# Decoder of four layers on one core: context block of the latent attentions padded to full height, and a new order of ranking, loads, output ring and final sums in the two mixture stages

## Chip, core and metric

One core of a Trainium2 chip runs the whole program in one launch. The metric is the device time in microseconds. TensorE (PE) multiplies, VectorE (DVE), ScalarE (ACT) and GpSimd (POOL) work on rows in SBUF and PSUM, and SyncE (SP) issues most of the loads; GpSimd issues the indirect transfers.

## The reference, cut to what matters

The residual x has 4 batches of 512 tokens with 256 features. It passes twelve stages, four layers of attention, cross-attention and feed-forward, each of the form x = x + f(layernorm(x)). Three of them (the cross-attentions of layers 1, 2 and 3; 16, 16 and 8 heads of 64) let the tokens attend to themselves and to 64 rows of context:

```
kv = concat([tokens, context]) @ Wkv          # 512 + 64 rows
attn = softmax(q @ k.T)                       # 512 x 576 per head and batch
out  = attn @ v                               # the product at issue in the first part of the change
```

Two of them (the feed-forward of layers 2 and 3) are mixtures of eight experts with two experts for each token:

```
gate = sigmoid or softmax of the two best of 8 router scores
h    = relu(x W1)^2                 # layer 2: 512 hidden features
h    = silu(x W1 + b1) * (x W2 + b2)  # layer 3: 512 + 512 up features, with biases
out  = sum over the two experts of gate * (h W_down [+ b3])
```

## The kernel before

**Stages.** Each stage is one block in which every engine runs its own written-out program; the engines meet only through semaphores, and a stage begins when all engines have left the one before. Stage 4, 7 and 10 (function `latent_attention`) take about 605 to 1341, 1950 to 2737 and 3149 to 3593 us of the profile; stages 8 and 11 (`sparse_experts`, called by `l2_ffn` and `l3_ffn`) take 2737 to 3000 and 3593 to 3940 us.

**Latent attention.** For each batch and each pair of heads (80 pairs in the three stages: 32, 32 and 16) TensorE does four "spots" of 128 query rows. In a spot it multiplies scores (L2491, rows of 64, so tiles of 64x128), transposes the shares of an earlier spot (L2411, L2423), and does one piece of other work: values (L2346), output projection (L2358), or `attended` (L2441, L2444). `attended` sums shares times values over five blocks of keys: blocks 0 to 3 hold 128 tokens each, and each of the two heads writes 64 of the 128 rows of PSUM bank 6 (tiles of 128x64, L2441). The fifth block is the 64 rows of context. `turn_context_probs` has put the shares of head 0 on partitions 0 to 63 and those of head 1 on 64 to 127 of `pTc`, and `vc` (context_values) holds the values the same way, so each head multiplies 64 rows by 64 columns (tiles of 64x64, L2444). In the trace each multiplication in float32 is two records (two passes). The order is part 0: blocks 0 and 1; part 1, one spot later: blocks 2, 3 and the context. The values in `vc` are copied by ScalarE at L2583.

**Mixture stages.** The tokens are 16 tiles of 128: group 0 has 4 tiles and group 1 has 12. Each group is ranked by itself: `pick` marks the two best experts (DVE), `rank` counts places with matmuls on PE (L4376, L4378), `put` makes the row indices and the expert of each sorted tile (DVE), `weigh` the gates. GpSimd then scatters the normed rows into DRAM by expert (`scatter`, L4298: 8 transfers for group 0 and 24 for group 1). SP loads the sorted rows back in chunks of three tiles (`load_sorted`, L4264; for a group it waits for that group's scatters at L4257 to L4260). There are 46 sorted tiles in each stage, 15 of group 0 and 31 of group 1. For tile n TensorE does `project_up(n)` (L4404, 16 records in layer 2, 32 in layer 3), `project_down(n-1)` (L4420) and `turn_rows(n+2)` (L4390). ScalarE moves turned rows (L4482), copies the expert's up weights out of the stage's weights (`copy_weights`, L4494) and applies relu or silu. DVE squares or multiplies (`make_hidden`) and moves the result into a ring `y` of RY = OUTPUT_RING = 4 row buffers (`make_rows`, L4678, L4681); GpSimd scatters a ring entry to the token's place (`scatter_rows`, L4307) and tells it by `stored`. While group 1 is being scattered, one `scatter_rows` stands behind every three scatters of rows, 8 in all. `rank(1)` stands on PE after `project_up(1)`, and `put(1)`, `weigh(1)` on DVE after `make_hidden(1)`, ahead of `make_rows(0)`. `pick(1)` is ahead of the loop.

**Loads.** SP issues the router, five small tables, the bias columns (layer 3), the up weights (4 MB in layer 2, 8 MB in layer 3), the stage's rows (layer 3: the down bias, 1 MB) and the down weights (4 MB), and only then waits for the scatters. DVE waits for both biases ahead of its loop.

**End.** When all 46 tiles are stored, SP fetches the expert outputs back (L4269; one batch earlier in the loop, three at the end), and `combine` adds the two halves of each token tile with two DVE instructions in a row (L4686, L4689), 12 tiles at the end. In layer 3 the result is stored by batch.

## Time and profile before

| what | value |
|---|---|
| time, median of 3 runs | 3911.28 us (3911.06 to 3914.19) |
| the profiled execution | 3942.55 us |
| its span | 3940.4 us, granted TensorE clock 0.929 |
| busy: PE / DVE / ACT / POOL | 3495.3 / 2191.8 / 1495.8 / 1370.0 us |
| PE busy, stage 4 from 656 to 1335 us | 657.24 of 679 us |
| stage 8 | 2737 to 3000 us |
| stage 11 | 3593 to 3940 us |

A row of the timeline gives start, length, engine, line, operation, the tiles written and read, the number of records merged (x) and in brackets how long the engine had been idle and what ended it. PEclk in the table by windows is the granted clock as a share of 2.4 GHz: 1.00 is 2.4 GHz and 0.50 is 1.2 GHz. "issue" and "remote" name idle time for which the profile shows no partner.

### The profile page before, as it was taken

Reading aid. Unit: us, or ns where it says so; the run is one execution under the profiler, and the core shown is the slowest. Engines: PE = TensorE matmul, PEld = TensorE weight load, DVE = VectorE, ACT = ScalarE, POOL = GpSimd, SP = SyncE. Lnnn points to the kernel's source line nnn. Section 1 sums busy time; section 2 is a strip of 40 time slices with the busy share of each in tenths; the row PEclk is TensorE's granted clock in tenths of the full one; section 3 lists DMA queues with packets and bytes.
Section 4 is the critical chain, followed back from the end, with each engine's and each line's share of the span. In section 5 each row is a group of like instructions: output and inputs, shape, how many; then the busy total and the mean of one; then the engine's idle time right before and its main releaser. Section 6 shows DMA issues by size and latency. Waiting matters only on the chain. (4 is left out here: it accounts for less than half of the span.)

```text
span 3940.4 us, 54458 instructions
## 1 busy us (share of the span) xinstructions
PE 3495.3 (89%) x18930; PEld 2240.6 (57%) x18930; DVE 2191.8 (56%) x5367; ACT 1495.8 (38%) x3040; POOL 1370.0 (35%) x1904
## 2 busy tenths in 40 slices
PE   7998897899999977888798999998896989995997
PEld 5675684445555566344444555555794445554896
DVE  5374444645556468666367676765234466664454
ACT  3253112433434364233244444443352144442453
POOL 2141441423323255232254444533422144442311
PEclk9999978999999988899799999999798889996998
DMA  2004001000000000000100000001221000003212
GB/s 100 1 1 123 14 1 46 1 1 1 1 1 1 13 1 24 1 1 1 49 1 1 1 1 1 1 1 76 99 80 57 4 25 1 1 1 160 71 60 84
DMA packets 48718, 108.85 MB, mean 28 GB/s; under 512 B 6660, under 2 KB 32900, under 8 KB 46404
## 3 DMA queue, kind: packets, MB, share of 16 engines
q1 hardware_dynamic: 40964, 84.88, 6.3%
q0 software_dynamic: 7488, 20.49, 1.5%
q8 instruction: 158, 2.59, 0.3%
q14 instruction: 108, 0.88, 0.1%
HBM read 70.67 MB, written 34.68 MB: 27 GB/s over the span
## 5 line engine op out<-in xcount | busy, mean ns | idle before, releaser
L2653 POOL TENSOR_SCALAR probs<-probs,inv_sum 128x512 f32<-128x512 f32 x640 | 437.7, 697 | 1008.3 <-DVE inv_sum L2774 1008.1
L2616 ACT ACTIVATE probs<-psum_banks,neg_max 128x576 f32<-128x576 f32 x640 | 468.5, 737 | 742.5 <-DVE neg_max L2857 742.5
L2857 DVE TENSOR_REDUCE neg_max<-psum_banks 128x1 f32<-128x576 f32 x640 | 455.0, 752 | 213.4 <-PE psum_banks L2491 206.8
L2491 PE MATMUL psum_banks<-keys_T,queries_T 64*128 64x288 f32 x2560 | 406.0, 436 | 52.5 <-ACT probs L2616 43.2
L2783 DVE COPY probs_T<-psum_banks 128x512 f32<-128x512 f32 x640 | 409.2, 681 | 4.5 <-PE psum_banks L2411 4.5
L2491 PEld LDWEIGHTS psum_banks<-keys_T,queries_T 64*128 64x128 f32 x2560 | 224.5, 189 | 269.2 <-ACT probs L2616 147.9
L2411 PE MATMUL psum_banks<-ident,probs 128*128 128x128 f32 x2560 | 356.5, 283 | 3.2 <-POOL probs L2653 2.3
L2411 PEld LDWEIGHTS psum_banks<-ident,probs 128*128 128x128 f32 x2560 | 280.3, 143 | 128.2 <-POOL probs L2653 63.3
L2441 PE MATMUL psum_banks<-probs_T,values 128*64 128x512 f32 x1280 | 310.9, 607 | 2.2 <-issue 2.2
L4404 PE MATMUL psum_banks<-sorted_T,tile_weights 128*128 128x128 f32 x2208 | 270.1, 279 | 9.2 <-ACT tile_weights L4494 4.9
L4404 PEld LDWEIGHTS psum_banks<-sorted_T,tile_weights 128*128 128x128 f32 x2208 | 262.2, 196 | 10.7 <-issue 10.6
L2853 DVE TENSOR_TENSOR psum_banks<-psum_banks,key_mask 128x128 f32<-128x128 f32 x192 | 57.5, 299 | 280.1 <-PE psum_banks L2491 280.1
L4420 PE MATMUL psum_banks<-w_L_experts_down,hidden_T 128*128 x736 | 183.3, 394 | 19.4 <-DVE expert_rows L4678 8.7
L4307 POOL DMA_INDIRECT expert_outputs<-expert_rows,output_index x92 | 90.3, 982 | 297.4 <-DVE expert_rows L4681 126.7
L2665 POOL TENSOR_TENSOR square_sum<-square_sum,neg_half 128x8 f32<-128x8 f32 x102 | 167.1, 1639 | 70.8 <-DVE square_sum L2749 69.3
L4420 PEld LDWEIGHTS psum_banks<-w_L_experts_down,hidden_T 128*128 128x128 f32 x736 | 137.4, 197 | 37.7 <-issue 21.7
L2346 PE MATMUL psum_banks<-w_L_xattn_Wkv,batch_normed_T 128*128 128x512 f32 x320 | 158.7, 620 | 0.0
L2441 PEld LDWEIGHTS psum_banks<-probs_T,values 128*64 128x64 f32 x1280 | 78.8, 136 | 133.8 <-issue 124.1
L4494 ACT COPY tile_weights<-w_L_experts_up 128x1024 f32 (+1 forms) x92 | 135.3, 1472 | 23.5 <-issue 23.5
L1962 ACT ACTIVATE probs_T<-psum_banks 128x512 f32<-128x512 f32 (+3 forms) x128 | 83.0, 701 | 127.7 <-PE psum_banks L1899 126.9
L2656 POOL TENSOR_TENSOR context_probs<-probs,inv_sum 128x128 f32<-128x128 f32 x320 | 128.9, 403 | 0.0
L2616 ACT ACTIVATION_READ_ACCUMULATOR probs<-psum_banks,neg_max 128x1 f32 x640 | 125.4, 196 | 0.0
(535 smaller groups left out, 6119.2 us busy)
## 6 DMA issues: line engine op xcount, KB each, us to landing
normed<-sorted_rows SPq DMA_DIRECT2D x30, 385.5 KB
sorted_rows<-zero_rows SPq DMA_DIRECT2D x8, 1028.0 KB, 14.5
w_L_experts_down<-in_L_experts_down SPq DMA_DIRECT2D x2, 4096.0 KB, 37.1
normed<-expert_outputs SPq DMA_DIRECT2D x8, 1024.0 KB, 7.9
w_L_xattn_Wkv<-in_L_xattn_Wkv SPq DMA_DIRECT2D x2, 2048.0 KB, 8.5
w_L_experts_up<-in_L_experts_up SPq DMA_DIRECT2D x1, 4096.0 KB, 13.0
sorted_rows<-zero_rows SPq DMA_DIRECT2D x4, 899.5 KB, 14.1
x_res<-in_x SPq DMA_DIRECT2D x4, 512.0 KB, 6.9
```

Source lines behind the costliest of these rows:

```text
L2346: last = pe.matmul(k.ps[:, 7, :], rows, wkv[:, c, W + a * 512:W + (a + 1) * 512], start=c == 0, stop=c == KC - 1)
L2411: last = pe.transpose(k.ps[:, 4 + n % 2, c * P:(c + 1) * P], prob[:, (b * NS + s) % PB, at + c * P:at + (c + 1) * P], k.ident[:, :])
L2441: last = pe.matmul(k.ps[r, 6, :], values[:, b % VB, c, (2 * j + h) * 64:(2 * j + h + 1) * 64], pT[:, q % 2, h, c, :], start=c == 0, stop=F ...
L2491: last = pe.matmul(k.ps[:, 2 * h + a, 0:HALF], qT[r, b % 2, j, t * P:(t + 1) * P], kT[r, j, k0:k0 + HALF], start=True, stop=True)
L2616: act.activation(prob[:, g % PB, h * w:(h + 1) * w].rearrange("p (a n) -> p a n", a=2), k.ps[:, 2 * h:2 * h + 2, 0:HALF], ACT.Exp, bias=nm ...
L2653: pool.tensor_scalar(w, w, inv[:, g % 4, h:h + 1], 1.0, ALU.mult, ALU.mult).then_inc(shared, 1)
L2665: pool.tensor_tensor(ss[:, i % 4, 2, :], ss[:, i % 4, 1, :], k.half[:, 0:8], ALU.pow).then_inc(inverted, 1)
L2783: dve.tensor_copy(pT[:, q % 2, h, :, t * P:(t + 1) * P], k.ps[:, 4 + n % 2, :].rearrange("p (c q) -> p c q", q=P)).then_inc(copied, 1)
L2857: dve.tensor_reduce(nmax[:, g % 4, h:h + 1], k.ps[:, 2 * h:2 * h + 2, 0:HALF], AX.XY, ALU.max, negate=True).then_inc(maxed, 1)
L4404: last = pe.matmul(ps[:, 2 * (n % 2) + part, f * P:(f + 1) * P], wt[:, n % 2, c, part * 512 + f * P:part * 512 + (f + 1) * P], xsT[:, n % ...
L4420: last = pe.matmul(ps[:, 6, 0:D], h[:, n % 2, f * P:(f + 1) * P], w_down[:, f // F, f % F * D:f % F * D + (E - 1) * STEP + D][:, bass.ds(a ...
L4494: act.copy(wt[:, n % 2, :, :], w_up[:, :, 0:(E - 1) * STEP + UP][:, :, bass.ds(at, UP)]).then_inc(weights_copied, 1)
```

## The change

In the latent attentions `vc` gets a second copy for each head, of full height: `vc[:, h]` holds the context values of head h on its own 64 partitions and zeros on the other 64. Two DVE memsets write the zeros at the start of the stage, and PE waits once for them. The context is then multiplied like the other blocks: all 128 rows of `pTc` against `vc[:, h]`.

In the mixture stages: `rank(1)` follows `project_up(0)`; `put(1)` follows `make_hidden(0)`; `weigh(1)` follows `make_rows(1)`. ScalarE copies the weights of tiles 0 and 1 ahead of the sigmoid or exp of group 1. The ring has six buffers. In layer 3 SP issues the down bias and the down weights behind the first two loads of sorted rows, and the waits for the biases stand at their first use. In the 12 sums at the end DVE adds the first half, ScalarE scales the second half in place and GpSimd adds it.

```diff
-        vc = k.sb("context_values", [P, PAIRS, NC], st)
+        vc = k.sb("context_values", [P, 2, PAIRS, NC], st)
...
+                        if q == 0:
+                            pe.wait_ge(zeroed, 2)
...
-                                last = pe.matmul(k.ps[r, 6, :], vc[r, j, :], pTc[r, q % 2, :], start=False, stop=True)
+                                last = pe.matmul(k.ps[r, 6, :], vc[:, h, j, :], pTc[:, q % 2, :], start=False, stop=True)
...
-                            act.copy(vc[r, 4 * a:4 * a + 4, :], k.ps[r, 7, :].rearrange(
+                            act.copy(vc[r, h, 4 * a:4 * a + 4, :], k.ps[r, 7, :].rearrange(
...
                 batch_aggr(0)
+                for h in range(2):
+                    dve.memset(vc[64 - 64 * h:128 - 64 * h, h, :, :], 0.0).then_inc(zeroed, 1)
                 dve.wait_ge(ctx_loaded, 16)
...
-OUTPUT_RING = 4
+OUTPUT_RING = 6
...
-                    sp.dma_start(columns[:, :, :, :], columns.src[:, :, :, :]).then_inc(bias_loaded, 16)
+                    sp.dma_start(columns[:, :, :, :], columns.src[:, :, :, :]).then_inc(columns_loaded, 16)
                 sp.dma_start(w_up[:, :, :], w_up.src[:, :, :]).then_inc(up_loaded, 16)
-                for w in k.stage_rows:
-                    sp.dma_start(w.dst[:, :], w.src).then_inc(bias_loaded, 16)
-                sp.dma_start(w_down[:, :, :], w_down.src[:, :, :]).then_inc(down_loaded, 16)
+                def load_late_weights():
+                    for w in k.stage_rows:
+                        sp.dma_start(w.dst[:, :], w.src).then_inc(bias_loaded, 16)
+                    sp.dma_start(w_down[:, :, :], w_down.src[:, :, :]).then_inc(down_loaded, 16)
+                if bias is None:
+                    load_late_weights()
...
                 load_sorted(0)
                 load_sorted(1)
+                if bias is not None:
+                    load_late_weights()
...
                 for n in range(done, NTILES):
                     scatter_rows(n)
+                for t in range(TT, NT):
+                    pool.wait_ge(halfway, t + 1)
+                    pool.wait_ge(second_scaled, t - TT + 1)
+                    pool.tensor_tensor(k.x[:, t, :], k.x[:, t, :], got[:, t - TT, 1, :], ALU.add).then_inc(combined, 1)
...
                     if n < NTILES:
                         project_up(n)
-                    if n == 1:
+                    if n == 0:
                         rank(1)
...
                 for p in range(1, PIECES):
                     move_piece(p)
+                copy_weights(0)
+                copy_weights(1)
                 if from_sigmoid:
...
                 move_rows(0)
                 move_rows(1)
-                copy_weights(0)
-                copy_weights(1)
...
+                for t in range(TT, NT):
+                    act.wait_ge(fetched[t // TT], 16)
+                    act.mul(got[:, t - TT, 1, :], got[:, t - TT, 1, :], gate[:, 1, t:t + 1]).then_inc(second_scaled, 1)
...
+                    if t >= TT:
+                        return
                     dve.wait_ge(halfway, t + 1)
...
-                if bias is not None:
-                    dve.wait_ge(bias_loaded, 32)
...
-                    if n == 1:
+                    if n == 0:
                         put(1)
-                        weigh(1)
                     if n >= 1:
                         make_rows(n - 1)
+                    if n == 2:
+                        weigh(1)
```

## Rows read from the trace of the kernel before

**Rows 1.** Timeline of PE, stage 4: part 0, then part 1 of `attended`

```profile
1011.31 1.94 PE L2441 MATMUL psum_banks<-probs_T,values 128*64 128x512 f32 x8
1013.18 1.24 PE L2491 MATMUL psum_banks<-keys_T,queries_T 64*128 64x288 f32 x8
...
1017.10 1.94 PE L2441 MATMUL psum_banks<-probs_T,values 128*64 128x512 f32 x8
1018.96 1.08 PE L2444 MATMUL psum_banks<-context_probs_T,context_values 64*64 64x512 f32 x4
1019.97 1.24 PE L2491 MATMUL psum_banks<-keys_T,queries_T 64*128 64x288 f32 x8
```

**Rows 2.** Timeline of PE, stage 10: sixteen passes of 512 columns with one tile shape

```profile
3262.65 7.13 PE L2369 MATMUL psum_banks<-w_L_xattn_Wq,batch_normed_T 128*128 128x512 f32 x16
```

**Rows 3.** Waits of PE, stage 4 (us in total, times, longest)

```profile
PE psum_banks L2491 <- ACT probs L2616: 14.1, 9, 2.4
```

**Rows 4.** Timeline of DVE: start of stage 4, and a memset in stage 8

```profile
609.38 1.40 DVE L2822 BATCH_NORM_STATS2 context_stat<-probs_T 64x6 f32<-64x256 f32 x4 [1.87 <-DMA probs_T<-in_ctx_rows]
...
2741.83 0.14 DVE L4619 MEMSET gate_row<- 128x96 f32 x1
```

**Rows 5.** Timeline of POOL and SP: last scatter of group 0, first sorted load, stages 8 and 11

```profile
2764.98 0.97 POOL L4298 DMA_INDIRECT sorted_rows<-normed,row_index  x1 [0.30 <-issue]
2767.80 50.04 SPq L4264 DMA_DIRECT2D normed<-sorted_rows  x5
...
3621.01 0.97 POOL L4298 DMA_INDIRECT sorted_rows<-normed,row_index  x1 [0.30 <-issue]
3635.36 78.42 SPq L4264 DMA_DIRECT2D normed<-sorted_rows  x6
```

**Rows 6.** Stage 11 by windows: stretch, length, busy of PE, PEld, DVE, ACT, POOL, PEclk, DMA share, GB/s

```profile
3630.00:3634.00 4.00, 0.00 (x0) 0.00 (x0) 0.00 (x0) 0.00 (x0) 0.00 (x0) 0.50 0.57 229
```

**Rows 7.** Timeline of ACT and PE: exp of group 1, first tiles of stage 11

```profile
3629.41 0.28 ACT L4476 ACTIVATE gate_exp<-gate_exp 128x96 f32<-128x96 f32 x1 [7.67 <-DVE gate_exp L4550]
3638.68 0.66 PE L4390 MATMUL psum_banks<-ident,normed 128*128 128x128 f32 x2 [13.31 <-DMA normed<-sorted_rows]
3643.26 5.49 PE L4404 MATMUL psum_banks<-sorted_T,tile_weights 128*128 128x128 f32 x32 [2.76 <-ACT tile_weights L4494]
...
3666.57 4.07 PE L4404 MATMUL psum_banks<-sorted_T,tile_weights 128*128 128x128 f32 x32
```

**Rows 8.** Timeline of PE, stage 8: first tiles, then two steady starts

```profile
2774.98 3.75 PE L4404 MATMUL psum_banks<-sorted_T,tile_weights 128*128 128x128 f32 x16 [2.13 <-ACT tile_weights L4494]
...
2781.35 2.76 PE L4378 MATMUL psum_banks<-gate_mask,ones 128*128 128x96 f32 x24
...
2790.64 3.77 PE L4420 MATMUL psum_banks<-w_L_experts_down,hidden_T 128*128 x8 [2.69 <-DVE expert_rows L4678]
...
2794.64 3.01 PE L4404 MATMUL psum_banks<-sorted_T,tile_weights 128*128 128x128 f32 x16
...
2813.55 1.95 PE L4404 MATMUL psum_banks<-sorted_T,tile_weights 128*128 128x128 f32 x16
...
2817.29 1.95 PE L4404 MATMUL psum_banks<-sorted_T,tile_weights 128*128 128x128 f32 x16
```

**Rows 9.** Timeline of ACT, stage 8, while group 1 is scattered

```profile
2803.28 0.60 ACT L4509 ACTIVATE hidden_T<-psum_banks 128x512 f32<-128x512 f32 x1 [6.73 <-remote]
```

**Rows 10.** Timeline of DVE and POOL: last sums of the program, and additions elsewhere

```profile
3925.20 0.48 DVE L4686 SCALAR_TENSOR_TENSOR x_res<-normed,gate_weights,x_res 128x256 f32<-128x256 f32 x1 [8.84 <-DMA normed<-expert_outputs]
...
3935.81 0.48 DVE L4689 SCALAR_TENSOR_TENSOR x_res<-normed,gate_weights,x_res 128x256 f32<-128x256 f32 x1
...
541.75 1.31 DVE L3316 SCALAR_TENSOR_TENSOR x_res<-projected,out_rstd,x_res 128x256 f32<-128x256 f32 x2
...
545.01 0.64 POOL L3185 TENSOR_TENSOR keys_decayed<-keys_decayed,gate_products 128x256 f32<-128x256 f32 x1
...
602.65 1.67 DVE L3316 SCALAR_TENSOR_TENSOR x_res<-projected,out_rstd,x_res 128x256 f32<-128x256 f32 x4 [0.17 <-DVE projected L3308]
```

More of the change, by code:

```diff
@@ L2267, in latent_attention @@
         with signals(nc, "ctx_stat", "ctx_aggr", "ctx_shift", "ctx_rstd", "ctx_normed", "ctx_turned", "ctx_ready",
-                     "ctx_loaded", "mask_made", "stats", "aggr", "shift", "rstd", "normed", "norm_turned", "norm_moved",
+                     "ctx_loaded", "mask_made", "zeroed", "stats", "aggr", "shift", "rstd", "normed", "norm_turned", "norm_moved",
                      "made", "act_moved", "dve_moved", "squared", "summed", "floored", "inverted", "scaled", "turned",
                      "moved", "placed") as (
-                ctx_stat, ctx_aggr, ctx_shift, ctx_rstd, ctx_normed, ctx_turned, ctx_ready, ctx_loaded, mask_made, stats, aggr,
+                ctx_stat, ctx_aggr, ctx_shift, ctx_rstd, ctx_normed, ctx_turned, ctx_ready, ctx_loaded, mask_made, zeroed, stats, aggr,
                 shift, rstd, normed, norm_turned, norm_moved, made, act_moved, dve_moved, squared, summed, floored,
@@ L4217, in sparse_experts @@
                      "router_loaded", "small_loaded", "up_loaded", "bias_loaded",
-                     "down_loaded", "next_ids") as (
+                     "down_loaded", "next_ids", "columns_loaded") as (
                 stats, aggr, shift, rstd, offset, normed, ids_set, copied_again, turned, ready, scored, rowed, picked,
                 exped, masked, ranked, indexed, placed, order, router_loaded, small_loaded, up_loaded, bias_loaded,
-                down_loaded, next_ids), signals(
+                down_loaded, next_ids, columns_loaded), signals(
                 nc, "sorted_0", "sorted_1", "ids_spared", "ids_taken", "x_turned", "x_moved", "up", "up_linear",
                 "shifted", "silued", "linear_read", "hidden_made", "weights_copied", "down", "rows_made", "combined",
-                "halfway", "x_stored", *[f"fetched_{b}" for b in range(B)]) as (
+                "halfway", "second_scaled", "x_stored", *[f"fetched_{b}" for b in range(B)]) as (
                 sorted_0, sorted_1, ids_spared, ids_taken, x_turned, x_moved, up, up_linear, shifted, silued, linear_read,
-                hidden_made, weights_copied, down, rows_made, combined, halfway, x_stored,
+                hidden_made, weights_copied, down, rows_made, combined, halfway, second_scaled, x_stored,
                 *fetched), nc.Block() as block:
@@ L4468, in _ @@
                                    scale=rs[:, 1, t:t + 1]).then_inc(normed, 1)
-                for p in range(1, PIECES):
-                    move_piece(p)
-                if from_sigmoid:
-                    act.wait_ge(scored, PIECES)
-                    act.activation(row[:, tiles_of[1], 0:E], scores[1], ACT.Sigmoid).then_inc(rowed, 1)
-                else:
-                    act.wait_ge(picked, 2)
-                    act.activation(e[:, tiles_of[1], :], e[:, tiles_of[1], :], ACT.Exp).then_inc(exped, 1)
                 def move_rows(n):
@@ L4495, in copy_weights @@
                         weights_copied, 1)
+                for p in range(1, PIECES):
+                    move_piece(p)
+                copy_weights(0)
+                copy_weights(1)
+                if from_sigmoid:
+                    act.wait_ge(scored, PIECES)
+                    act.activation(row[:, tiles_of[1], 0:E], scores[1], ACT.Sigmoid).then_inc(rowed, 1)
+                else:
+                    act.wait_ge(picked, 2)
+                    act.activation(e[:, tiles_of[1], :], e[:, tiles_of[1], :], ACT.Exp).then_inc(exped, 1)
                 move_rows(0)
                 move_rows(1)
-                copy_weights(0)
-                copy_weights(1)
                 for n in range(NTILES):
@@ L4652, in make_hidden @@
                         return
+                    if n == 0:
+                        dve.wait_ge(columns_loaded, 16)
                     at = dve.value_load(bias_at[0:1, 0, n:n + 1], min_val=0, max_val=(E - 1) * 8)
@@ L4679, in make_rows @@
                     else:
+                        if n == 0:
+                            dve.wait_ge(bias_loaded, 16)
                         at = dve.value_load(bias_at[0:1, 1, n:n + 1], min_val=0, max_val=(E - 1) * D)
@@ L4698, in _ @@
                         make_hidden(n)
-                    if n == 1:
+                    if n == 0:
                         put(1)
-                        weigh(1)
                     if n >= 1:
                         make_rows(n - 1)
+                    if n == 2:
+                        weigh(1)
                     if GROUP_SORTED[0] + 10 <= n < GROUP_SORTED[0] + 10 + TT:
```

## The prediction

> **What bounds the kernel now.** I first looked for the stages that the change touches, then asked in each which engine has no idle time. In the latent attentions TensorE bounds: its timeline goes from one product to the next without a bracket [rows 1], and its longest wait in stage 4, for ScalarE's exponentials, is 14.1 us in 9 places [rows 3], nearly all at the start of a batch. A microsecond of TensorE is there a microsecond of the stage. In the mixture stages I read three stretches apart. At the start, TensorE waits for the sorted rows and then for the first weight copies [rows 5, 7, 8]. In the middle it is the bound again, with a start of `project_up` every 2817.29 - 2813.55 = 3.74 us in stage 8 [rows 8]; in stage 11, which has twice the up products, a tile should take 5.52 us (3.74 us and 16 more records of an up product, which take 1.95 us less a pipe's length of 0.17). Only while group 1 is scattered does it stand still here and there. At the end DVE alone adds 12 tiles, (3935.81 + 0.48) - 3925.20 = 11.1 us [rows 10], with every other engine idle.
>
> **The context as a fifth block.** The number of matmuls, their columns and their passes stay the same; what changes is the tile shape of the last two passes, from 64x64 to the 128x64 of the eight records before. Part 1 now takes 1019.97 - 1017.10 = 2.87 us from its start to the next score: 1.86 us for the four paired passes and 1.01 us for the two of the context [rows 1]. Passes of 512 columns in one shape cost at most 7.13 / 16 = 0.446 us each [rows 2], and part 0, four such passes and one change of shape, takes 1.87 us [rows 1]. Part 1 after the change is part 0 and two passes more: 1.87 + 2 x 0.43 = 2.73 us (0.43 is 7.13 less a pipe's length of 0.6, over 15). That is 0.14 to 0.15 us less per pair, and 80 pairs give 12 us. Part 1 stands in the longest spot of its four, so the exponentials of that spot have more time than elsewhere and the gain should not turn into a wait; if every one of the shortened spots were held up by the exponentials instead, about a third would stay. Bounds 4 to 13, value **-12.0 us**. The zeros: a memset of 96 columns takes 0.14 us [rows 4], and one of 512 columns at the same rate at most 5 times that, 0.7 us. Both lie in front of DVE's wait for the context load, 1.87 us long [rows 4], so they cost **nothing**; were the load early they would cost up to 1.4 us a stage. The wait of TensorE for them is over 50 us late by then.
>
> **Stage 8, start.** The first up product waits 2.13 us for the weight copies behind the two moved rows [rows 8]. The copies need `placed(0)` and the up weights, both there before the sigmoid of group 1, so they move into ScalarE's idle time and the product begins when the second tile is turned: **-2.1 us** (0 if the copies were late).
>
> **Stage 8, second ranking.** `put(1)` and `weigh(1)` on DVE stand in front of `make_rows(0)`, for which the second down product waits 2.69 us [rows 8]. The idle time costs twice: behind it that down product takes 3.77 us and the up product 3.01 us, against 1.95 us for an up product in the steady stretch [rows 8], the clock having fallen from 2.4 to 1.2 GHz. From the first up product to the fourth it is 2794.64 - 2774.98 = 19.7 us [rows 8]. After the change the order is up 0 (3.75 less the pipe, 3.55, at 1.2 GHz as now), ranking (2.8 [rows 8], and 0.6 of slow clock), a turn (0.2), and two steady tiles (2 x 3.74), in all 14.6 us. `put(1)` is 16 small DVE instructions of 0.2 to 0.4 us, 3.6 us from the ranking's end; TensorE has up 1 and down 0 to do meanwhile, 3.6 us, and `make_rows(0)` is needed only for down 1. `weigh(1)`, 2.3 us behind `make_rows(1)`, meets the up product of tile 3. So nothing new is late: **-5.0 us** (bounds 2.7, the idle time alone, and 5.9, idle time and slow records).
>
> **Stage 11, start.** This is the largest term. In stage 8 the first sorted load is issued 2767.80 - 2764.98 = 2.8 us after the last scatter of group 0 began; in stage 11 it takes 3635.36 - 3621.01 = 14.35 us [rows 5]. In between the DMA engines still move 229 GB/s while every compute engine stands still [rows 6]: up weights, row biases and down weights, 13.4 MB, are ahead. Without the last two, 5.2 MB or two fifths of it, some 14 of the 38 us of traffic go, and the load should be issued 2.8 us after the last scatter as in stage 8, at 3623.8, its rows on chip 3.3 us later (3638.68 - 3635.36 [rows 5, 7]), at 3627.1. Then something else is last: `move_rows` stands behind the exp of group 1, whose input comes from DVE, and which ends at 3629.7 [rows 7]. From there it is a move and the second turn, 1.1 us, to an up product at 3630.8 instead of 3643.26 [rows 7]. The copies of 1.9 us each are hidden before the exp. **-12.4 us**, and -6 if the scatters still land half as late as now. What is moved: the two late loads go behind two waits of SP, and land at about 3624.9 + 14 = 3639; down 0 comes at 3630.8 + 5.3 + 2.8 + 0.2 + 3.6 = 3642.7, 4 us later. No other load waits behind them before tile 6.
>
> **Stage 11, second ranking.** From the first to the fourth up product 3666.57 - 3643.26 = 23.3 us [rows 7]; after the change 5.3 (the 5.49 us of up 0 less the pipe) + 2.8 + 0.2 + 2 x 5.52 = 19.4 us: **-3.9 us** (bounds 2.2 and 4.1).
>
> **Ring of six.** In neither stage does DVE wait for a buffer now: while group 1 is scattered GpSimd needs 4 x (0.97 + 0.30) = 5.1 us for each ring entry [rows 5], DVE hands one over at that pace or slower. It would matter only if TensorE ran through the scatters undisturbed at 3.74 us a tile. **0** (bound: -5).
>
> **The stretch of the scatters.** ScalarE stands still up to 6.73 us with all its inputs there [rows 9], and the tiles of this stretch lose some 19 us in stage 8 and 8 us in stage 11 against the steady pace. What it waits for the profile doesn't show, and the change takes none of these transfers away, so I leave it at **0**, with -15 and +10 as bounds, since other instructions will meet the scatters.
>
> **Sums on three engines.** DVE's part falls to 0.42 us a tile, but GpSimd's addition of a tile takes 0.64 us alone [rows 10]. Side by side they are not free: two DVE additions that meet GpSimd's take 1.31 us where four alone take 1.67 us [rows 10], so one of them was held up by 0.47 us. If they take turns throughout it is 12 x (0.42 + 0.64) = 12.7 us against 11.1, +1.5 us a stage; if they overlap, 0.5 + 12 x 0.64 = 8.2, -2.9 us. I take the first, as both rows' lengths speak for it: **+3.0 us** for both stages (bounds -5.8 and +4.6).
>
> The Trainium skill (SBUF — State Buffer, "SBUF: two separate sides") says that an addition of VectorE with two inputs in SBUF and any GpSimd instruction hold a shared port for the whole instruction and exclude each other. The stretched rows agree; by it and GpSimd's longer additions the sum would be about a microsecond a stage worse.
>
> **Sum.** -12.0 - 2.1 - 5.0 - 12.4 - 3.9 + 3.0 = -32.4 us. The profiled execution has 3942.55 us, 2.15 more than its span and 31.3 more than the median; its forecast is 3910. The terms are intervals between waits and not shares, so I take them from the median as they are: 3911.3 - 32.4 = 3878.9.
>
> **Rivals.** (a) The late weights are not what holds the scatters. Each scatter would then land as late as now, and stage 11 would gain only the hidden copies, 2.8 us [rows 7], instead of 12.4: 3888.5. For it: GpSimd's scatters are another queue. Against it: 14.35 against 2.8 us with the same eight scatters [rows 5], and an end that comes with the end of the traffic [rows 6].
>
> By the Trainium skill (DMA: Bandwidth & Descriptors, "Queues, rings and completion order") a DMA engine takes its queues in turn, packet by packet. With equal turns a scatter would not be held by the weights, which is this rival; the 14.35 us speak against it, unless a turn of the weights moves much more than one of the scatter.
>
> (b) The stalls in the scatters belong to the old order and go: another 15 to 25 us, 3859. For it: TensorE will be ahead by then. Against: ScalarE's 6.73 us have no partner in the old order either.
> (c) The latent attentions turn the gain into waits for the exponentials: 3887.
> (d) Slower: with six buffers TensorE runs ahead of GpSimd's 5.1 us a tile in stage 8, and idles in every tile until the clock falls to 1.2 GHz for the stretch, as behind the 2.69 us of rows 8. A tile then takes 7.5 instead of 3.74 us, and 12 tiles cost 45 us: 3924. [...]
> (e) The sums overlap fully: 3870.
>
> **How the numbers follow.** Forecast 0.55, (a) 0.10, (b) 0.12, (c) 0.10, (d) 0.03, (e) 0.07, the rest (a smaller gain from several bounds at once, within 7.8 us of before) 0.03. The range takes in (a), (c), (e) and the edge of (b), and the open stretch of the scatters: 3860 to 3896. Within 0.2%, 7.8 us, a measurement of this kernel can't tell a change. Faster 0.94, same 0.03, slower 0.03.
>
> **What would show it.** One kind of tile 128x64 in `attended` and 2.7 us from part 1 to the next score; the first sorted load of stage 11 some 3 us after the last scatter began; no wait of 2 us at the second down product; up 0 directly behind the second turn; GpSimd's additions at the end stretched to 1 us or more. Wrong it would be if TensorE showed new waits for L2616 in the latent attentions, if down 0 of stage 11 waited for its weights, or if the scatters' stalls moved onto TensorE's path.

## The result, and the profile after

The changed kernel takes 3895.01 us (median of 5 runs, 3892.15 to 3897.32), the kernel before in the same runs 3914.19 us (3911.06 to 3918.84): a ratio of 0.9949, 95% interval 0.9938 to 0.9960, or 19.2 us less. The forecast was 32.4 us less. The range (3860 to 3896) held by 1 us, the size was 13 us too large, and this part is mostly about these 13 us.

The profiled execution of the changed kernel took 3895.01 us and spans 3893.3. That of the kernel before spans 3940.4, so the two traces are 47 us apart and the medians 19. This is the first thing to explain. The page after begins so (section 1 is busy time by engine, then the granted clock in 40 slices):

```profile
span 3893.3 us, 54516 instructions
PE 3471.5 (89%) x18930; PEld 2243.6 (58%) x18930; DVE 2192.1 (56%) x5349; ACT 1506.5 (39%) x3064; POOL 1392.1 (36%) x1928
...
PEclk9999978999999988899889999999898889997998
```

**Latent attentions.** Timeline of PE in stage 4, against [rows 1]. Part 1 now lasts 1015.50 - 1012.77 = 2.73 us up to the next score, the forecast 2.73; the wait for the exponentials is unchanged from [rows 3]:

```profile
1012.77 1.94 PE L2443 MATMUL psum_banks<-probs_T,values 128*64 128x512 f32 x8
1014.54 1.03 PE L2446 MATMUL psum_banks<-context_probs_T,context_values 128*64 128x512 f32 x4
1015.50 1.24 PE L2493 MATMUL psum_banks<-keys_T,queries_T 64*128 64x288 f32 x8
...
PE psum_banks L2493 <- ACT probs L2618: 14.1, 9, 2.4
```

The zeros take 0.48 us each on DVE, and the wait for the context behind them, 1.87 us in [rows 4], still has 0.46 us left, so they cost nothing (timeline of DVE, stage 4):

```profile
607.88 0.48 DVE L2823 MEMSET context_values<- 64x512 f32 x1 [0.16 <-issue]
608.83 1.40 DVE L2826 BATCH_NORM_STATS2 context_stat<-probs_T 64x6 f32<-64x256 f32 x4 [0.46 <-DMA probs_T<-in_ctx_rows]
```

**Stage 8.** Timeline of PE, against [rows 8]. The first up product follows the second turn, the ranking comes behind it, and the waits of 2.13 and 2.69 us are gone. But at tile 15, the first of group 1, there is a new wait for the sorted rows, and the up product behind it takes 3.23 us in place of 1.95:

```profile
2764.36 0.69 PE L4405 MATMUL psum_banks<-ident,normed 128*128 128x128 f32 x2 [0.46 <-ACT sorted_T L4488]
2764.84 3.62 PE L4419 MATMUL psum_banks<-sorted_T,tile_weights 128*128 128x128 f32 x16
2768.26 0.59 PE L4391 MATMUL psum_banks<-gate_mask,w_before_token 128*128 128x104 f32 x2
...
2824.00 0.69 PE L4405 MATMUL psum_banks<-ident,normed 128*128 128x128 f32 x2 [3.75 <-DMA normed<-sorted_rows]
2824.48 3.23 PE L4419 MATMUL psum_banks<-sorted_T,tile_weights 128*128 128x128 f32 x16
```

That load is issued when the scatters of group 1 have landed, and POOL issued the last of them at 2817.70, one instruction every 1.28 us:

```profile
2816.42 0.98 POOL L4309 DMA_INDIRECT sorted_rows<-normed,row_index  x1 [0.30 <-issue]
2817.70 0.97 POOL L4309 DMA_INDIRECT sorted_rows<-normed,row_index  x1 [0.30 <-issue]
```

**Stage 11.** Timelines of POOL, SP, ACT and PE, against [rows 5, 7]. The first sorted load is issued 3596.53 - 3592.53 = 4.0 us after the last scatter of group 0, in place of 14.35; SP's wait for the scatters' landing, which ends just ahead of it, lasts 27.8 us in place of 37.2. The exp of group 1 is then last, and the move and the turn follow it; down 0, for the late weights, waits for nothing:

```profile
3592.53 0.98 POOL L4309 DMA_INDIRECT sorted_rows<-normed,row_index  x1 [0.30 <-issue]
3596.53 0.91 SPq L4273 DMA_DIRECT2D normed<-sorted_rows  x2
3602.72 0.28 ACT L4512 ACTIVATE gate_exp<-gate_exp 128x96 f32<-128x96 f32 x1 [4.08 <-DVE gate_exp L4568]
3603.32 0.69 PE L4405 MATMUL psum_banks<-ident,normed 128*128 128x128 f32 x2 [2.59 <-ACT sorted_T L4488]
3603.80 6.13 PE L4419 MATMUL psum_banks<-sorted_T,tile_weights 128*128 128x128 f32 x32
3616.42 1.89 PE L4435 MATMUL psum_banks<-w_L_experts_down,hidden_T 128*128 x8
```

**The sums.** End of stage 8: timelines of DVE and POOL, then what the sequencers recorded where the stage's block ends (columns: instruction, count, duration in ns as minimum, median and maximum, first and last start in us), then SP's first load of stage 9:

```profile
2957.22 9.53 DVE L4708 SCALAR_TENSOR_TENSOR x_res<-normed,gate_weights,x_res 128x256 f32<-128x256 f32 x12 [9.05 <-DMA normed<-expert_outputs]
2957.88 10.14 POOL L4359 TENSOR_TENSOR x_res<-x_res,normed 128x256 f32<-128x256 f32 x12 [7.90 <-ACT normed L4530]
...
L4231 POOLq DRAIN  x1: 7678/7678/7678, 2966.8 to 2966.8; - x1
L4231 DVEq DRAIN  x1: 17/17/17, 2968.3 to 2968.3; - x1
L4231 SPq EVENT_SEMAPHORE  x1: 17/17/17, 2974.6 to 2974.6; - x1
...
2975.72 0.35 SPq L3902 DMA_DIRECT2D w_L_attn_w_q<-in_L_attn_w_q  x1
```

The sums end at 2968.0, 10.8 us after their start, against 11.1 us in [rows 10]. The next stage begins 7.7 us later. In between POOL executes one DRAIN of 7.68 us. It stands behind the last addition in POOL's program and begins at 2966.8. The instruction is in the kernel before too. There it begins right behind the last scatter and is over before DVE has added its first tile, which began at 2987.4 (the same view of the kernel before, end of stage 8):

```profile
L4227 POOLq DRAIN  x1: 7635/7635/7635, 2979.2 to 2979.2; - x1
L4227 DVEq DRAIN  x1: 17/17/17, 2998.8 to 2998.8; - x1
```

### The profile page after: what moved, and what is told of

Same layout as the page of the kernel before. It is cut to its first block and busy times, and to the rows that moved or that the text cites. A ratio compares the mean times of both kernels' runs of the same rounds, so it can differ in the third digit from the quotient of the medians.

```text
span 3893.3 us, 54516 instructions
## 1 busy us (share of the span) xinstructions
PE 3471.5 (89%) x18930; PEld 2243.6 (58%) x18930; DVE 2192.1 (56%) x5349; ACT 1506.5 (39%) x3064; POOL 1392.1 (36%) x1928
## 5 line engine op out<-in xcount | busy, mean ns | idle before, releaser
L4435 PE MATMUL psum_banks<-w_L_experts_down,hidden_T 128*128 x736 | 174.3, 380 | 2.2 <-DVE expert_rows L4703 1.4
## 6 DMA issues: line engine op xcount, KB each, us to landing
w_L_experts_up<-in_L_experts_up SPq DMA_DIRECT2D x1, 4096.0 KB, 12.2
```

Source lines behind the costliest of these rows:

```text
L4435: last = pe.matmul(ps[:, 6, 0:D], h[:, n % 2, f * P:(f + 1) * P], w_down[:, f // F, f % F * D:f % F * D + (E - 1) * STEP + D][:, bass.ds(a ...
```

## The experiments

The runs come in four groups, each on another chip (in this order those numbered 9, 4, 12 and 10). In the second and fourth the kernel before took 3914 us, in the first and third 3942 and 3939. I call these places B and A; the medians on record belong to B, the profiled execution of the kernel before to A. What in the chips differs isn't shown.

I measure a stage by its length, from SP's first load of it to SP's first load of the next (rows are shown for two kernels below). All in us:

```
kernel                    place  stage 4  7      10     8      11     whole, median
before (first profile)    A      735.3  787.4  444.1  262.8  346.9
before again              A      735.3  787.4  444.1  262.9  346.0  3940.98
context alone             A      730.7  782.3  439.7  262.5  345.5  3929.12
late loads alone          A      735.0  786.8  444.2  262.7  334.9  3929.86
late loads alone          B      735.3  786.8  444.4  241.8  329.3  3900.30
second ranking alone      A      738.0  786.8  439.5  255.7  337.9  3927.50
changed kernel            B      731.1  782.4  439.9  246.7  328.4  3894.17
 ring of four             B      730.7  782.3  440.1  245.9  328.2  3895.87
 sums on one engine       B      730.7  782.7  440.3  242.9  322.8  3888.25
 ranking as before        B      730.2  783.0  440.1  250.5  333.2  3907.88
 loads as before          A      730.6  782.9  440.0  261.2  340.7  3927.51
 one engine, sparser rows A      730.7  782.6  440.8  259.3  338.2  3914.52
```

**1. The kernel before again: are the stalls one execution's?** No edit.

> The kernel before, unchanged, profiled a second time. Theory S (the stalls without a partner in the scatter stretches, about 19 us in stage 8 and 8 us in stage 11, belong to the one profiled execution and not to the ordinary ones): this profile's span is 3910 to 3918 us, its stage 8 lasts some 244 to 247 us where the first profile had 262.75, its stage 11 some 338 where it had 346.9, and its up projections in the scatter stretch follow one another without gaps. Rival R (the stalls belong to the kernel before and the change removed them): the second profile shows stages 8 and 11 at about 262 and 347 us again. Ratio to itself 1.000 for both.

3940.98 us, ratio to itself 0.9994 (0.9985 to 1.0004). The stalls are there again, in the same places and sizes; timeline of ACT in stage 8 of this run, against [rows 9]:

```profile
2804.65 0.60 ACT L4509 ACTIVATE hidden_T<-psum_banks 128x512 f32<-128x512 f32 x1 [7.08 <-remote]
2830.43 0.37 ACT L4482 COPY sorted_T<-psum_banks 128x256 f32<-128x256 f32 x1 [4.35 <-remote]
```

So theory S falls, and rival R looked right. But here the timed runs were 3941 us too. Neither theory had thought of that: the stalls go with where the kernel is run.

**2. The context block alone.** On the kernel before:

```
-        vc = k.sb("context_values", [P, PAIRS, NC], st)
+        vc = k.sb("context_values", [P, 2, PAIRS, NC], st)
...
-    last = pe.matmul(k.ps[r, 6, :], vc[r, j, :], pTc[r, q % 2, :], start=False, stop=True)
+    last = pe.matmul(k.ps[r, 6, :], vc[:, h, j, :], pTc[:, q % 2, :], start=False, stop=True)
```

> The kernel before with the padded context block of the latent attentions alone. Forecast step: -12.0 us (ratio 0.9969, bounds -4 to -13). Theory M (the attentions gave what was forecast, the shortfall lies in the mixture stages): -11 to -13 us, that is ratio 0.9967 to 0.9972. Rival (part of the attention's gain is given back in the stages behind it): -5 to -8 us, ratio 0.9980 to 0.9987.

Ratio 0.9967 (0.9954 to 0.9979), 13.0 us less. Stages 4, 7 and 10 are 4.6, 5.1 and 4.4 us shorter, 14.1 in all. Theory M holds.

**3. The late loads alone, in both places.**

```
+                def load_late_weights(): ...
                 load_sorted(0)
                 load_sorted(1)
+                if bias is not None:
+                    load_late_weights()
```

> The kernel before with the bias rows and the down projection's weights of stage 11 issued behind the first two sorted loads, alone. Forecast step: -12.4 us (ratio 0.9968). The two profiles show 11.0 us from the stage's start to the first up product, some of it from the earlier copies of the weights: -9 to -12 us by them, ratio 0.9970 to 0.9977. Rival (in ordinary executions the scatters land sooner than in the profiled one, so that less was to be gained): -3 to -6 us, ratio 0.9985 to 0.9992.

Ratio 0.9971 (0.9959 to 0.9983), 12.2 us less, in A. The first up product of stage 11 comes 39.9 us after the stage's start in place of 49.8. That is 9.9 us; what lies between it and the last down product is 2.2 us shorter as well (269.5 against 271.7), for which no cause is shown.

> The kernel before with the late loads of stage 11 alone, a second time. Where the kernel before takes 3914 us: its stage 8 is the unchanged one, and by the kernel with the old ranking (250.5 us) less the 6.1 us that the drain cost there it should last 244 to 245 us, so that the changed kernel's 246.7 us are 2 us more than before; its stage 11 should last 329 to 331 us (333.2 less the 3.7 us of the drain) against some 341 without the late loads, and the whole should come out 10 to 13 us below the kernel before. Rival (the step is worth less without the stalls): 4 to 8 us below. Where the kernel before takes 3940 us: 12 us below, as in the first run of this kernel, with stage 11 at 335 us.

Ratio 0.9970 (0.9958 to 0.9982), 14.2 us less, in B. The step is worth the same in both places, and this kernel shows what the places differ in. Its stage 8, which the edit doesn't touch, lasts 2997.98 - 2735.29 = 262.7 us in A and 2974.75 - 2732.92 = 241.8 us in B (timelines of SP, first A, then B):

```profile
2735.29 0.33 SPq L4242 DMA_DIRECT2D w_L_ffn_router_w<-in_L_ffn_router_w  x1
2997.98 0.35 SPq L3898 DMA_DIRECT2D w_L_attn_w_q<-in_L_attn_w_q  x1
```

```profile
2732.92 0.33 SPq L4242 DMA_DIRECT2D w_L_ffn_router_w<-in_L_ffn_router_w  x1
2974.75 0.34 SPq L3898 DMA_DIRECT2D w_L_attn_w_q<-in_L_attn_w_q  x1
```

The waits of ACT from 2780 to 2850 us, in the stretch of the scatters, are these (us in total, times, longest), A and then B; the two "remote" lines of A have no counterpart in B:

```profile
ACT hidden_T L4516 <- remote: 10.8, 2, 6.7
ACT sorted_T L4489 <- remote: 5.1, 1, 5.1
ACT tile_weights L4501 <- issue: 2.5, 9, 0.5
```

```profile
ACT sorted_T L4489 <- PE psum_banks L4397: 31.4, 18, 5.7
ACT tile_weights L4501 <- issue: 5.5, 17, 0.5
```

20.9 us in stage 8 and 5.6 us in stage 11 are 26.5 of the 28.4 us between the two spans of this kernel. The 47 us between the profiles of before and after are these stalls and the change. I had expected 244 to 245 us for stage 8; it is 241.8, which makes the changed kernel's stage 8 (246.7) 4.9 us *longer* than before in the place where the times were taken.

**4. The second ranking alone, and taken back.** On PE `if n == 1: rank(1)` became `if n == 0:`, on DVE `put(1)` moved ahead of `make_rows(0)` and `weigh(1)` to n == 2, on ACT the first two copies of the weights ahead of the exponentials.

> The kernel before with the second ranking behind the first up products and the weights' first two copies ahead of it, alone, in both mixture stages. Forecast steps: -2.1 -5.0 -3.9 = -11.0 us (ratio 0.9972). Theory W (the scatters of the second group end at a time that their own queue sets, so that work brought ahead of them is given back in the wait of the first sorted load of the second group, 3.75 us in stage 8 of the changed kernel): -3 to -7 us, ratio 0.9982 to 0.9992. Rival (the gain is whole and the shortfall is in the sums or the ring): -9 to -12 us.

Ratio 0.9964 (0.9952 to 0.9976), 14.6 us less, in A. That is more than either theory gave, and theory W's 3 to 7 us don't hold here. Stage 8 is 7.1 us shorter, as forecast, and stage 11 is 9.0 us shorter, where the expectation counted 3.9: it had left out the copies hidden ahead of the exponentials (2.8 us by the prediction's rival (a); the first up product does come 2.1 us earlier), and the rest is 6.7 us shorter. The stages that weren't touched move too (stage 10 by -4.6 us, stage 4 by +2.7, what lies ahead of it by +5.5), and in A stalls fill the stretch in which theory W has its wait.

> The changed kernel with the second ranking, the second exponentials and the first copies of the weights back at their old places. Forecast step: 11.0 us more than the changed kernel (-2.1 -5.0 -3.9 undone). Theory W (in the changed kernel the first sorted load of the second group waits 3.75 us for its scatters, in stage 8, and gives a part back): 3 to 8 us more. Alone on the kernel before it gave -14.6 us.

3907.88 us, 13.7 more than the changed kernel, in B. Of these only 3.7 and 4.8 us lie in stages 8 and 11; some 6 us lie ahead of stage 4, where nothing is edited, so the whole time can't be read here. In B the kernel of experiment 3 tells what the move does in stage 8. With the old order its first up product begins 37.7 us after the stage's start and its last down product ends at 219.9; with the new order (the changed kernel's second profile, experiment 7) it is 35.6 and 218.8. The start gains the 2.1 us of the forecast; what lies between lasts 182.1 us in the old order and 183.2 in the new. But these two kernels differ in the ring as well. With the ring of four in both (experiment 5 has the new order) it is 182.1 and 182.1 us, with the ring of six in both (this run has the old order) 183.6 and 183.2. So the new order gives 0 to 0.5 us of the forecast 5.0, and three profiles of the new order with six buffers (182.9, 183.2 and, in experiment 6, 185.6) scatter by more than that. The turn of tile 15 shows why the gain is missing. In the old order (timelines of PE and POOL, stage start 2732.92):

```profile
2830.61 0.38 PE L4397 MATMUL psum_banks<-ident,normed 128*128 128x128 f32 x2
...
2823.21 0.97 POOL L4305 DMA_INDIRECT sorted_rows<-normed,row_index  x1 [0.30 <-issue]
```

TensorE arrives 97.7 us after the stage's start and waits for nothing. The last scatter is issued at 90.3 us, in the new order at 88.6 (2817.70 - 2729.09, the first profile of the changed kernel). There the rows are on chip at 94.9 us (2824.00 - 2729.09), and TensorE would be ready at 91.2. So of the 7.1 us of the forecast 97.7 - 94.9 = 2.8 are kept, and the slow up product behind the wait takes 1.3 of these. In stage 8 of B theory W holds, and more strongly than I had put it.

**5. The ring of four in the changed kernel.** `OUTPUT_RING = 4`.

> The changed kernel with its output ring back at four buffers. Forecast step: the ring gives 0 (bound -5), so the kernel of four takes the same time as the changed kernel, within 2 us. Rival (the ring of six is what keeps the scatter stretch free of stalls): 5 to 28 us more than the changed kernel.

3895.87 us, 1.7 more than the changed kernel; the intervals (0.9948 to 0.9975 against 0.9941 to 0.9969) don't tell them apart, and stages 8 and 11 are 0.8 and 0.2 us shorter. Stage 8, waits of PE and then of DVE (us in total, times, longest):

```profile
PE psum_banks L4435 <- DVE expert_rows L4698: 4.1, 4, 1.1
PE psum_banks L4405 <- DMA normed<-sorted_rows: 1.5, 2, 1.0
...
DVE expert_rows L4698 <- DMA expert_outputs<-expert_rows,output_index: 12.1, 4, 4.1
```

With four buffers DVE does wait for the ring and TensorE for DVE, three times 1.1 us; in return the wait at tile 15 falls to 0.5 us. Both rings come to nearly the same point, the landing of the last scatter: tile 15 is turned 95.1 us after the stage's start with six buffers and 96.0 with four. The ring gives nothing, as forecast, but not because nobody waits for it; what lies between the first up and the last down product of stage 8 is even 1.1 us longer with six buffers (183.2 against 182.1), which is less than the 2.4 us by which experiment 6 differs there from the changed kernel without an edit in that stretch.

**6. The sums on VectorE alone.** The POOL and ACT loops of the change are left out and DVE does both additions.

> The changed kernel with the final sums back on VectorE alone. Forecast step: the three engines cost +3.0 us in both stages together (bounds -5.8 and +4.6), so that this kernel takes 3 us less than the changed kernel. By the profile of the changed kernel, in which the sums last 10.8 us instead of 11.1 in each stage, it takes 0.6 us more.

3888.25 us, ratio to the kernel before 0.9938 (0.9924 to 0.9951), 5.9 us *less* than the changed kernel; all five runs (3885.5 to 3889.1) lie below all five of the changed kernel (3891.4 to 3896.8). The same views of this kernel at the end of stage 8:

```profile
L4231 POOLq DRAIN  x1: 7635/7635/7635, 2949.7 to 2949.7; - x1
L4231 DVEq DRAIN  x1: 17/17/17, 2969.3 to 2969.3; - x1
...
2970.54 0.35 SPq L3902 DMA_DIRECT2D w_L_attn_w_q<-in_L_attn_w_q  x1
```

The drain is as long, but it begins behind the last scatter and ends at 2957.3, before the sums start. From the last down product's end to the stage's end it is 21.9 us here (242.9 - 221.0), 22.0 in the kernel before with late loads, and 28.0 in the changed kernel. In stage 11 it is 25.3, 25.4 and 28.9; there the last stores hide a part. The step costs 9.5 us in both stages, by these ends. The whole shows only 5.9, since other things moved: stages 8 and 11 are 9.4 us shorter together, but what lies between the first up and the last down product of stage 8 is 2.4 us longer, and stage 6, which no edit touches, 5.1 us. My second expectation, +0.6, came from reading the additions alone.

One part of stage 11's gain isn't the step's. Its first up product comes at 36.95 us here and at 38.8 in the changed kernel, because the router products, some 20 us after the stage's start, ran at a granted clock of 1.00 here and of 0.50 there, and DVE's value for the exp waits for the last of them (timelines of PE, the changed kernel's first profile, then this one):

```profile
3585.28 3.58 PE L4382 MATMUL psum_banks<-w_L_ffn_Wg,normed 128*128 128x8 f32 x16 [0.95 <-ACT normed L4468]
```

```profile
3581.08 1.95 PE L4378 MATMUL psum_banks<-w_L_ffn_Wg,normed 128*128 128x8 f32 x16 [0.95 <-ACT normed L4464]
```

The clock of this stretch doesn't go with the edits: it is 0.50 in experiment 2 as well, whose stage 11 is that of the kernel before, and 1.00 in all three profiles of the kernel before.

**7. The changed kernel again.**

> The changed kernel itself, timed beside the kernel before in the runs of this call. The kernel before took 3914 us where the change was first timed and 3942 us where its parts were timed alone (-13.0, -12.2, -14.6 us, together -39.8). Theory K (the stalls in the scatter stretches, 28 us, depend on where a kernel is run and not on the kernel; the parts lose some of their worth to one another): the changed kernel takes 18 to 25 us less than the kernel before wherever it is run (3917 to 3924 us where the kernel before takes 3942). Rival V (the stalls go with the change as a whole where there are any): 38 to 48 us less where the kernel before takes 3942 (3894 to 3904 us), and 19 us less where it takes 3914.

3894.17 us, ratio 0.9955 (0.9941 to 0.9969), 19.6 less, in B, so this run can't tell K from V. The kernel with the old loads, run in A, can: its stage 8 is that of the changed kernel and lasts 261.2 us, against 246.7 in B. So the stalls don't go with the change, and V falls. How much the whole change gives in A was not measured.

**8. Three more runs in A.**

> The kernel before, unchanged, profiled where the kernel before takes about 3914 us (if it takes 3942 us here, this run tells only that the stalls are there again). Theory P (the 28 us between 3942 and 3914 us are the stalls of the scatter stretches and nothing else): stage 8 lasts 243 to 247 us in place of 262.8, stage 11 some 337 to 340 in place of 346.9, all other stages as in the first profile within 2 us for each 4 us of half clock. Rival: stages 8 and 11 last 262 and 346 us here too and the 28 us lie in other stages.

3941.0 against 3938.94 us, 262.5 and 348.8 us: the run fell in A and tells only that the stalls are there a third time. The question was settled by experiment 3.

> The changed kernel with the bias rows and the down projection's weights of stage 11 loaded at their old place, ahead of the sorted loads. Forecast step: 12.4 us more than the changed kernel. Alone on the kernel before the step gave -12.2 us and stage 11 went from 346.0 to 334.9 us, in a place with the stalls. Theory (the step is whole wherever it is run): 10 to 13 us more, all of it in stage 11 (338 to 341 us where the changed kernel has 328.4). Rival (part of it was a stall that went away with it): 4 to 8 us more.

3927.51 us, ratio to the kernel before 0.9970 (0.9959 to 0.9981). The changed kernel wasn't run in A, so the 10 to 13 us can't be read from the whole. The first up product of stage 11, a place that the stalls don't reach (39.9 us in A and B in experiment 3), comes 47.8 us after the stage's start against 38.8 in the changed kernel: 9.0 us, what is left of the step when the copies are hoisted already.

> A version that should beat both kernels: the changed kernel with the final sums on VectorE alone, so that POOL's closing drain of 7.6 us lies beside the wait for the last rows and the sums instead of behind them, and with a row scatter after every fourth instead of every third scatter of the second group. Against the kernel with the sums on VectorE alone (3888 us where the kernel before takes 3914, stage 8 at 242.9 us, wait of PE for the first sorted load of the second group 4.0 us): two row scatters of 1.28 us fewer ahead of that load, so that the wait falls to 1.3 to 1.7 us and stage 8 to 240 to 241 us; 3885 to 3887 us in all, ratio to the kernel before 0.992 to 0.9935. Rival (the row ring of six then holds VectorE up): stage 8 at 243 to 246 us and stage 11 up as well.

```
-                    if t % 3 == 0:
+                    if t % 4 == 3:
                         scatter_rows(done)
```

3914.52 us against 3938.94, ratio 0.9935 (0.9923 to 0.9947), 24.4 less. It is faster than the kernel before, but whether the sparser rows do anything stays open. In A the stalls hold TensorE up (waits of PE in stage 8), so it comes to tile 15 when the rows are there already, and the wait that the edit should have shortened doesn't occur:

```profile
PE psum_banks L4431 <- issue: 10.9, 2, 6.1
PE psum_banks L4415 <- issue: 4.7, 7, 1.1
```

The version that beats both kernels, measured in B, is that of experiment 6: the change with the sums left on VectorE.

## Why the prediction was right, and where its size was off

The terms, in B where there are two kernels to compare (kernel before with late loads, and changed kernel), in us:

```
step                        forecast  measured  from
latent attentions           -12.0     -13.2     stages 4, 7, 10: -4.3 -4.4 -4.5 (alone: -13.0)
zeros                         0         0       0.46 us of the wait left
stage 8, start               -2.1      -2.1     37.7 to 35.6
stage 8, second ranking      -5.0       0.0     182.1 to 182.1, both with a ring of four
stage 11, start             -12.4     -11.0     49.8 (before, in A) to 38.8
stage 11, second ranking     -3.9      -3.3     263.9 to 260.6
ring of six                   0        +1.1     182.1 to 183.2, stage 8, both in the new order
stretch of the scatters       0         0       the times are from B, which has no stalls
sums on three engines        +3.0      +9.5     22.0 to 28.0, 25.4 to 28.9
sum                         -32.4     -19.0     medians: -19.2, -19.6
```

The measured terms come from single profiles, and stages that no edit touches differ between them by up to 8 us. That their sum meets the medians within 0.6 us is in part luck. So is the range: its slow end stood for rivals (a) and (c), which both fell, and it was reached by two costs that the prediction had not seen.

**Right, and for the reason given:** the context block (2.73 us a pair, and no new wait), the start of stage 8, and the late loads. The last rests on [rows 5, 6], and its rival (a) falls: the sorted load comes 4.0 us behind the last scatter, not 14.35. It was 1.4 us too large, since DVE's value for the exp came later (37.7 us after the stage's start, 35.9 in [rows 7]) and I had taken that end as fixed. It is the clock of the router products that moved it (experiment 6): where they ran at 2.4 GHz, the first up product comes at 36.95 us, 12.8 us earlier than before. Rival (c) falls with the unchanged wait of 14.1 us.

**The sums (6.5 us of the 13.4).** The step that failed is the one that compared durations of additions: 12.7 or 8.2 us against 11.1. Of the rows it rested on, the addition of POOL in [rows 10] (545.01) lies behind the stretched pair of DVE (541.75); the POOL instructions that do lie beside the pair are an addition from 541.12 to 542.03 and multiplications from 541.99 on. The additions do stretch each other (9.53 / 12 = 0.79 us a tile on DVE and 10.14 / 12 = 0.85 on POOL, where the forecast took 0.42 and 0.64 alone), yet the whole lasts 10.8 us, so that part was even too dark. What I left out is what follows POOL's last instruction in the stage, the drain of 7.6 us. It stood in the profile of the kernel before, in the rows of the sequencers at the block's end, which I hadn't read since they count as no busy time. With it the sum would have been +6 us in stage 8 and something less in stage 11. The upper bound of 4.6 us was too low for the same reason. The forecast cited the Trainium skill (SBUF — State Buffer, "SBUF: two separate sides"), by which the two engines' additions exclude each other on a shared port. For two-input additions of VectorE the section limits this to GpSimd instructions that read SBUF, which these additions do; the forecast's "any GpSimd instruction" was too wide. The stretched additions agree in kind; by full exclusion a tile would cost the 1.06 us of the forecast, and the measured 10.8 us for 12 tiles are less than that.

**Stage 8, second ranking (5.0 us, and 1.1 with the ring).** The mechanism was right: both waits and the slow products behind them went. The step that failed is "so nothing new is late". I followed the change through the first four tiles and not to the next point where TensorE meets another queue. That queue was POOL's: 24 scatters of rows with 7 of outputs between them at 1.28 us each, 42.5 us from the first to the last (46.1 to 88.6 us after the stage's start in the changed kernel), and 6.3 us more until the rows are on chip. In these 42.5 us POOL itself stands still once, 2.28 us, for its own first twelve scatters to land. Put against TensorE's pace, 15 tiles at 3.74 us, it is decided at tile 15, by 3.75 us. The profile of the kernel before couldn't warn of it, since in A some 19 us of stalls lie ahead of that tile: TensorE turns it 118.8 us after the stage's start, and its load, issued at 104.4, had waited for TensorE to free a buffer and not for the scatters. But the prediction itself said that the stalls might be gone, as rival (b), and left out that without them this wait is the next one. In stage 11, where a tile takes 5.52 us, TensorE comes to tile 15 later, no wait is there, and the same step gave 3.3 of 3.9 us.

**The median.** Taking the terms off the median "as they are" was right for most of them: late loads and context gave the same in both places. It was wrong for the term whose cover was a stall: by the new order what comes ahead of the last down product of stage 8 is 7.2 us shorter in A (experiment 4), and in B 1.6 us shorter with the ring of four and 3.7 with the ring of six. The difference of 31.3 us between the profiled execution and the median was in the prediction, but not asked after; nearly all of it was the stalls that [rows 9] shows.

**The other rivals.** (b) is half right: the 15 to 25 us are gone in the times, but in the times of the kernel before as well. (d), the slow one, had the right queue in view, POOL's pace in stage 8, and the wrong place: no idle time in every tile, but one wait of 3.75 us behind all of them. (e) isn't seen.

## What to carry to other kernels

Before an engine is given the last piece of a stage, read what its sequencer does between its last instruction and the barrier; an engine that has issued scatters may have several microseconds of draining to do, which are free only while somebody else works. When waits are taken out of the front of a stretch, follow the engine to the next point where it needs another queue, and compare both paces up to there: that balance is the ceiling of the gain. And when the profiled execution is longer than the median, find out first which rows hold the surplus, since a stall that the timed runs don't have can be the only cover of the next wait.

## What the runs showed of the hardware

- A DRAIN of POOL at the end of a mixture stage takes 7.63 to 7.68 us in every kernel here, whether it begins right behind the last scatter (2949.7, experiment 6) or behind twelve additions, some 17 us after it (2966.8, the changed kernel). What it does in that time the profile doesn't show.
- The same kernel runs 28 us apart on different chips. On 9 and 12 there are stalls of 4 to 8 us on ACT, DVE and PE at nearly the same points each time (three profiles of the kernel before, the chip of the first not on record), on 4 and 10 none (the changed kernel, and the kernel before with late loads). 26.5 of the 28.4 us lie in the two stages in which POOL scatters; the cause is open.
- Stages that no edit touches differ by up to 8 us between profiles (stage 5: 223.0 to 230.8 us). Stage 5 of the same kernel took 230.8 us at a mean granted clock of 0.84 in one profile and 226.7 at 0.86 in another, both mixtures of the levels of 1.2 and 2.4 GHz. The lengths of the mixture stages, in which one place stays within some tenths of a microsecond, told more than the whole (windows of the changed kernel, first profile and second; columns as in [rows 6]):

```profile
1335.85:1566.61 230.76, 186.31 (x1000) 149.70 (x1000) 159.13 (x982) 121.84 (x374) 107.08 (x60) 0.84 0.02 6
```

```profile
1336.00:1562.70 226.70, 181.31 (x1000) 145.41 (x1000) 159.00 (x982) 121.73 (x374) 106.99 (x60) 0.86 0.02 6
```
